# Segment sums of a graph network: two groups in TensorE's column halves, a staging bank, and placing in batches

## The reference

```python
agg_edge = jax.ops.segment_sum(edge_attr, dst, num_segments=12500)     # 12500 x 48
h0 = relu(layernorm(x))
collected = concatenate([h0, agg_edge], axis=1)                         # 12500 x 176
h = silu(collected @ W1 + b1)                                           # 256 wide
h = silu(h @ W2 + b2)
out = x + h0 + (h @ W3 + b3)                                            # 128 wide
```

## Time and profile before

| | |
|---|---|
| median of 3 runs | 367.58 us |
| lowest and highest run | 367.41 and 370.16 us |
| the profiled execution, its own time | 369.57 us |
| its span, first to last instruction | 367.8 us |
| TensorE busy (matmul, load) | 347.2 and 327.8 us |
| VectorE, ScalarE, GpSimd busy | 260.8, 203.1 and 32.6 us |
| moved by DMA | 52.96 MB |

### The profile page before, as it was taken

How to read it: one execution, slowest core, us unless ns; L and a number is a source line. 1 busy time by engine, 2 the same in 40 slices (tenths; PEclk the granted TensorE clock), 3 DMA queues, 4 the chain that set the end, 5 groups by cost and what they waited for, 6 DMA issues and landing times.

```text
span 367.8 us, 11752 instructions
## 1 busy us (share of the span) xinstructions
PE 347.2 (94%) x4336; PEld 327.8 (89%) x4337; DVE 260.8 (71%) x630; ACT 203.1 (55%) x377; POOL 32.6 (9%) x44
## 2 busy tenths in 40 slices
PE   1488999999999999999999999999999999999995
PEld 1387999999999999999999999999999999999994
DVE  6864866976687667866796669766876688666652
ACT  7543466555655566456645565556555654566471
POOL 4011101110111001110111011101110011101100
PEclk9996999999999999999999999999999999999999
DMA  4953756454555455455635554545554555551111
GB/s 136 295 158 83 219 152 177 131 167 134 175 134 165 127 173 168 131 138 172 182 115 152 165 174 123 169 133 175 137 163 127 172 153 149 138 170 28 27 27 47
DMA packets 78757, 52.96 MB, mean 144 GB/s; under 512 B 2482, under 2 KB 78348, under 8 KB 78738
## 3 DMA queue, kind: packets, MB, share of 16 engines
q1 hardware_dynamic: 78738, 52.70, 50.3%
HBM read 46.29 MB, written 6.40 MB: 143 GB/s over the span
## 4 chain that ended last, share of the span: by engine, by line
PE 93%; DVE 4%; issue 2%; POOL 1%; ACTq 0%; DVEq 0%; POOLq 0%; ACT 0%
PE agg_ps L836 41%; PE z L899 14%; PE z L880 7%; PE z L888 6%; PE z L882 6%; PE z L869 3%; PE z L864 3%; PE z L870 3%; PE z L865 3%; PE z L866 3%; PE tp L849 3%; DVE farthest L522 1%; PE z L774 1%; DVE window L505 0%; DVE rel_rows L518 0%
## 5 line engine op out<-in xcount | busy, mean ns | idle before, releaser
L836 PEld LDWEIGHTS agg_ps<-onehot,raw 128*48 128x48 f32 x3128 | 147.8, 128 | 7.3 <-issue 3.6
L836 PE MATMUL agg_ps<-onehot,raw 128*48 128x42 f32 x3128 | 151.1, 217 | 3.3 <-issue 3.3
L714 DVE TENSOR_TENSOR out_t<-z,resid 112x512 f32<-112x512 f32 (+1 forms) x28 | 19.4, 692 | 84.6 <-PE z L899 84.6
L558 DVE TENSOR_TENSOR onehot<-window,rel 128x1176 f32<-128x1176 f32 (+1 forms) x56 | 76.9, 1375 | 0.7
L425 ACT ACTIVATE xn<-x_t,nmr,rstd 112x128 f32<-112x128 f32 (+1 forms) x112 | 46.2, 483 | 36.6 <-DVE nmr L550 29.8
L899 PEld LDWEIGHTS z<-w,h 128*112 128x112 f32 (+1 forms) x448 | 51.7, 176 | 5.3 <-issue 4.5
L377 POOL TENSOR_TENSOR rstd<-vareps,minus_half 112x4 f32<-112x4 f32 (+1 forms) x28 | 28.2, 1008 | 312.0 <-DVE vareps L542 312.0
L899 PE MATMUL z<-w,h 128*112 128x128 f32 (+1 forms) x448 | 54.4, 274 | 0.9 <-ACT h L446 0.9
L446 ACT ACTIVATE h<-z,b2c 128x448 f32<-128x448 f32 (+1 forms) x56 | 32.4, 631 | 26.5 <-PE z L888 26.5
L880 PE MATMUL z<-h_hi,w_hi 128*128 128x448 f32 (+1 forms) x112 | 43.5, 389 | 0.0
L385 ACT ACTIVATE agg_ps<-zeros 48x512 f32<-48x512 f32 x28 | 16.5, 592 | 45.4 <-DVE agg_carry L668 45.4
(11 more groups left out here) (89 smaller groups left out, 341.4 us busy)
## 6 DMA issues: line engine op xcount, KB each, us to landing
raw<-in_edge_attr_dram SPq DMA_DIRECT2D x55, 672.0 KB, 4.6
x_t<-in_x_dram SPq DMA_DIRECT2D x27, 224.0 KB, 2.9
out_dram<-out_t SPq DMA_DIRECT2D x27, 224.0 KB, 2.5
dst_rows<-in_dst_dram SPq DMA_DIRECT2D x1, 768.0 KB
raw<-in_edge_attr_dram SPq DMA_DIRECT2D x1, 480.0 KB, 4.0
out_t<-in_L_gnn_W_dram SPq DMA_DIRECT2D x1, 256.0 KB, 7.0
x_t<-in_x_dram SPq DMA_DIRECT2D x1, 192.0 KB
out_dram<-out_t SPq DMA_DIRECT2D x1, 192.0 KB
```

Source lines behind the costliest of these rows:

```text
L558: return dve.tensor_tensor(onehot[:, slot, 0:n * PER, :], window[:, :].unsqueeze(1).broadcast_to([P, n * PER, WINDOW]), cols.unsqueeze(2). ...
L836: mm = pe.matmul(banks[0:ED, bass.ds(offsets[k], WINDOW)], raw[0:rows, slot, k, j, :], onehot[0:rows, slot, k * PER + j, :], start=False, ...
```

## The change

**Sums.** The matmuls of two neighbouring groups alternate, one writing partitions 0 to 47 and the other partitions 64 to 111 of a new PSUM bank `stage` (`tile_position` (0, 0) and (0, 64)). The 7 pairs of a tile lie side by side in it (7 x 42 columns). Their output addresses are fixed.

**Copy and placing.** ScalarE copies the bank to SBUF (`stage_sums`). TensorE then places each window: one fp32 matmul whose stationary operand is a 112 x 48 slice of the identity and whose moving operand is the staged pair, with the group's offset as output address (`place_batch`). A batch holds the last 3 groups of tile b-1 and the first 11 of tile b, so one wait for a cleared bank serves a batch.

**Order.** TensorE's step becomes: layer 1 of i-1, offsets and sums of i+1, layer 3 of i-2, transposes of i, placing of i+1, layer 2 of i-1. One pair of banks `z` serves layers 1 and 2, so layer 1 waits for the SiLU of the preceding layer 2, and layer 2's loops are turned (output half outside). ScalarE: relu, split_agg, clear_bank, activate2, activate1, normalize, stage_sums. VectorE's step is reordered, and its one-hots run two tiles ahead. SP loads edges three tiles ahead.

**Prologue.** The first destination of every group is loaded by itself, and row set 0 (the first 128 groups) goes through validity, offset, transposes, one-hots and the sums of tile 0 before row sets 1 to 3 are looked at. The formula of the offsets is shorter. TensorE runs 10 and 6 matmuls of the identity whose results nobody reads (`WARM0`, `WARM1`). Tiles 0 and 1 are summed and placed ahead of the loop, which now starts at step 1 and ends in a loop over 4 to 22.

The diff, cut to its core:

```diff
+    PAIRS = GPT // 2
+    STAGED = PAIRS * WINDOW
-    LOOP_FIRST, LOOP_END = 4, 24
+    LOOP_FIRST, LOOP_END = 4, 22
+    WARM0, WARM1 = 10, 6
...
+        staged = sb("staged", [ROW2 + ED, 2, PAIRS, WINDOW])
...
-        z1 = ps("z1", [P, M, BANK])
-        z2 = ps("z2", [P, M, BANK])
+        stage = ps("stage", [P, BANK])
+        z = ps("z", [P, M, BANK])
...
             def step(i, parity):
-                if has(i, -2, NT):
-                    load_edges(i + 2, parity, 0)
+                if has(i, -3, NT):
+                    load_edges(i + 3, 1 - parity, 0)
...
+            def stage_sums(t, parity):
+                act.wait_ge(s_summed, 2 * t + 2)
+                if not isinstance(t, int) or t > 1:
+                    act.wait_ge(s_placed, t)
+                act.activation(staged[:, parity].rearrange("d k w -> d (k w)"), stage[0:ROW2 + ED, 0:STAGED],
+                               ACT.Copy).then_inc(s_staged, 1)
...
             def step(i, parity):
                 if has(i, 1, NT):
                     relu(i - 1)
+                if has(i, 1, NT):
+                    split_agg(i - 1)
                 if has(i, 1, NT - 2):
                     act.wait_ge(s_carried, i)
                     clear_bank(1 - parity)
-                if has(i, 1, NT):
-                    split_agg(i - 1)
-                if has(i, 0, NT):
-                    normalize(i, parity)
                 if has(i, 2, NT):
                     activate2(i - 2)
                 if has(i, 1, NT):
                     activate1(i - 1)
+                if has(i, 0, NT):
+                    normalize(i, parity)
+                if has(i, -1, NT):
+                    stage_sums(i + 1, 1 - parity)
...
-                    for j in range(PER):
-                        mm = pe.matmul(banks[0:ED, bass.ds(offsets[k], WINDOW)],
-                                       raw[0:rows, slot, k, j, :], onehot[0:rows, slot, k * PER + j, :],
-                                       start=False, stop=True, skip_group_check=True)
+                    for j in range(PER):
+                        for side in range(2):
+                            half, k = divmod(2 * pair + side, HALF)
+                            if 2 * pair + side < total:
+                                rows = P if k < counts[half][1] else TAIL_P
+                                at = ROW2 * side
+                                mm = pe.matmul(stage[at:at + ED, pair * WINDOW:(pair + 1) * WINDOW],
+                                               raw[0:rows, 2 * parity + half, k, j, :],
+                                               onehot[0:rows, 2 * parity + half, k * PER + j, :],
+                                               start=(pair == 0 and j == 0), stop=True, skip_group_check=True,
+                                               tile_position=(0, at))
...
+            def place_batch(b, parity, offsets):
+                first, last = batch_of(b)
+                pe.wait_ge(s_staged, b + 1)
+                wait(pe, s_clear, b + 1)
+                for offset, k in zip(offsets, range(first, last)):
+                    group = k % GPT
+                    at = ROW2 * (group % 2)
+                    mm = pe.matmul(banks[0:ED, bass.ds(offset, WINDOW)], ident[0:ROW2 + ED, at:at + ED],
+                                   staged[:, parity if k >= 0 else 1 - parity, group // 2, :],
+                                   start=False, stop=True, skip_group_check=True)
+                    if k == EARLY - 1 and has(b, 1, NT):
+                        mm.then_inc(s_closed, 1)
+                mm.then_inc(s_placed, 1)
...
                 for m in range(M):
                     cols = slice(m * P, (m + 1) * P)
-                    pe.matmul(z1[:, m, 0:n], w1x_hi[:, cols], hT_hi[:, 0:n], start=True, stop=False)
+                    wait(pe, s_h2, M * (t - 1) + m + 1)
+                    pe.matmul(z[:, m, 0:n], w1x_hi[:, cols], hT_hi[:, 0:n], start=True, stop=False)
...
                 if has(i, -1, NT):
                     offsets = offsets_of(i + 1)
+                    sum_tile(i + 1, 1 - parity)
                 if has(i, 2, NT):
                     layer3(i - 2)
                 if has(i, 0, NT):
                     transposes(i, parity)
                 if has(i, -1, NT):
-                    sum_tile(i + 1, 1 - parity, offsets)
+                    place_batch(i + 1, 1 - parity, offsets)
                 if has(i, 1, NT):
                     layer2(i - 1)
```

## The result

| | before | after |
|---|---|---|
| median | 368.34 us (4 runs, those shown ahead among them) | 419.95 us (4 runs, 418.25 to 424.14) |
| span of the profiled execution | 367.8 us | 416.5 us |
| one step, mean of 25 | 12.02 us | 13.77 us |

The ratio is 1.141, with a 95% interval of 1.131 to 1.152: the changed kernel is 14% slower, where 352 us had been forecast, outside the range's upper end of 391.

What follows compares the result with a forecast made beforehand. TensorE's instructions were taken to bound the step: -0.42 us x 26 = -10.9, with -5.0 in the prologue, gave 353.7; the runs' median lying 2.0 lower made it 352 us, range 336 to 391.

Steps and rivals of the forecast that it cites:

- The sums: TensorE's 112 group-sum passes in overlapping column halves: 26 ns each instead of 45.2, saving 2.15 us a step.
- Rival A: At the sums, loads don't overlap between column halves: a pass stays 45.2 ns, kernel 407.6 us; chance 0.17.
- Rival B: At the sums, loads overlap but streams don't: a pass 36 to 42 ns, taken as 39, kernel 389.6 us; chance 0.09.
- Placing and the narrow form: On TensorE, 28 placing passes cost 1.27 us a step; entering and leaving the narrow form a second time adds 0.33.
- One pair of z banks: Layer 1 waits for the preceding layer 2's SiLU on the shared bank: 0.13 us a step, bounds 0 and 0.3.
- The offsets: A load of 1.3 to 3.4 us ahead of the sums, covered by layer 1's ten long queued passes as before.
- sum of a step: TensorE's step changes by -2.15 + 1.27 + 0.33 + 0.13 = -0.42 us, x 26 = -10.9 us.
- Rival C: Overlap holds but the step is stopped elsewhere, 0.4 us more a step; kernel 362.6 us; chance 0.11.
- The copy, ScalarE, VectorE, SP: ScalarE's stage copy takes 0.5 us, covered by layer 3 and the transposes; VectorE's one-hots and SP's loads are in time.
- Prologue: First sums near 11.3 us, layer 1 of tile 0 at 31 to 33; gain 5 us, bounds 1 and 9.
- two offset loads and the flag: In the prologue, between the transposes at 25.5 us and the placing: done at 27.
- the tail: From the last sums to the end: same layers, left at its length.

Runs made afterwards that it cites:

- e1: Changed kernel with every offset load begun 1 or 3 words earlier, at a multiple of 4 words: 363.43 us, ratio 0.988 to the kernel before.
- e5: Kernel before, with odd tiles' offsets loaded from two words earlier so every load starts at a multiple of four words: 362.81 us against 367.55, ratio 0.987.
- e12: Kernel before with only one wait added, layer 1's second half waiting for the SiLU of the preceding layer 2's first half: 406.62 us, ratio 1.107.
- e11: e7 with the offsets of tiles 0 and 1 loaded at the earliest prologue place and `clear_carry(1)` behind ScalarE's copies: 344.60 us, ratio 0.938.
- e3: Changed kernel with constant offsets for tiles 2 to 27, so no per-step loads or register work: 355.01 us, ratio 0.965 to the kernel before.
- e7: Changed kernel with offset loads aligned and ahead of layer 1, x issued first, and VectorE's nmr behind the first low part: 348.34 us, ratio 0.947.
- e2: Changed kernel with the unchanged offset loads placed ahead of layer 1 in TensorE's program: 392.49 us, ratio 1.066 to the kernel before.
- e9: e1 with VectorE making `nmr` ahead of the one-hots: 364.59 us, ratio 0.990 to the kernel before.

## Why the prediction was wrong

**The sums.** Right in mechanism and nearly in size. A pass in column halves costs 22.6 ns, exactly half of the 45.2 of the earlier trace rows, where I took 26; the block takes 2.65 us instead of 5.17, -2.52 against the -2.15 forecast. The floor of 25 ns that I took from the one-column loads is no floor for these. Rivals A and B, which held 26% between them, are both refuted. By the Trainium skill (TensorEngine Tiling (Array Packing), Key Properties) different tiles load and multiply at once, and the runs agree: 22.6 ns in two halves, 45.3 in one. The Trainium skill's page TensorE: Matmul & The Clock Gate, The mechanism, lets a load overlap running matmuls only when its row group differs. Here both groups use all rows and a pass still costs half, so the measurement decides against it for column halves. (Rival B's upper value was misreckoned: by its own slope 42 columns take 44.5 ns and not 42. It changes nothing here.)

**Placing and the narrow form.** 28 passes in 1.38 us, forecast 1.27. Both entries together cost 0.21 us a step more than before, forecast 0.33. Right.

**One pair of z banks.** Layer 1 follows layer 2 without a gap (109.12), the forecast was 0.13 us. As a delay of layer 1 the wait costs nothing. But it is the wait that did the damage elsewhere.

**The offsets.** This is the step that failed: the load "stands in front of the sums instead of layer 3; layer 1's ten long passes in the queue cover it as before". Each half of it was wrong.
- I had read 1332/2329/3370 as a spread. It is two values, by the place of the first word, and the new batches' start (14b - 3) leaves only the long one. e1 and e5 show it: 57 us (some 4.5 of them the slow steps) and 5 us. The median of 2329, between two clusters with nothing near it, was the sign.
- The cover is not "as before". A load covers itself only as far as the sequencer runs ahead, and the new `s_h2` wait at layer 1's second half stops it there: five passes (1.0 us) in front instead of seventeen (3.4). e12 shows it with that wait alone.

Together: 3.34 + 0.3 of register work behind it, less 1.0 of cover, is the 2.6 us of the timeline. With the short load 1.5 + 0.3 - 1.0 = 0.8 (e1: 0.7). My sum of a step had this term at nothing. The wait with short loads (e1) still leaves the kernel 1.2% faster than before. Long loads without the wait were not tried in the changed kernel: with one pair of banks it can't be left out. The odd tiles of the kernel before are such a case: a long load cost 0.19 us there (12.13 against 11.94, gone in e5). So either of the two alone costs little (0.19 us the long load, 0.5 to 0.7 us the wait in e1); the 2.6 us take both. Of the new wait I had asked only how long its own matmul stands, not which instruction behind it used to run early. Rival C did name "the sequencer held", though at the wait for the staged sums, and priced it at up to 0.4 us a step, by the tightness of my count and not by the longest thing behind the wait, 3.4 us in the earlier trace rows.

**The copy, ScalarE, VectorE, SP.** `staged` takes 0.416 us (forecast 0.5) and nobody waits for it. x lands later and `rstd` takes 2.06 us instead of 1.01; both were unforeseen and both are hidden.

**Prologue.** The first sums begin at 11.3, as counted (rows of their line, first and last start):

```profile
L919 PE MATMUL stage<-onehot,raw x3128: 208/213/306, 11.3 to 388.9; 128*48 128x42 f32 x195, 80*48 80x42 f32 x1
```

Then the chain of the changed kernel in order of time goes another way:

```profile
21.56 3.60 PE stage L919 x112
...
25.62 1.65 ACT xn L470 x4
...
27.32 1.01 PE tp L949 x4
28.33 5.06 issue
33.40 2.96 PE agg_ps L936 x34
```

The 5.06 us of "issue" are mostly two loads (1.52 and 3.34) that start only at 27.3, when the wait of the transposes for `xn` is met: the same hold again. I had given "two offset loads and the flag" 1.5 us. Layer 1 of tile 0 begins at 37.46, not at 31 to 33, and the gain of 5 us is not there. e11 loads before that wait: placing at 27.76 and layer 1 at 32.73, within the forecast, though at the low clock (0.50 from 28.6 to 35.3 us, 1.2 GHz). Its timeline:

```profile
27.76 4.22 PE L939 MATMUL agg_ps<-staged,ident 112*48 112x42 f32 x50 [0.49 <-issue]
32.73 0.71 PE L968 MATMUL z<-hT_hi,w1x_hi 128*128 128x448 f32 x1 [0.75 <-issue]
...
36.74 3.15 PE L922 MATMUL stage<-onehot,raw 128*48 128x42 f32 x112
```

**The total.** Rival A's time, 407.6, lay near the measured one, but its reason isn't there. With the stall taken out the kernel takes 355.0 us (e3) or 348.3 (e7), close to my 352, but part of that is luck. A step of e7 takes 11.04 us on the mean of 25, where I had 11.60, 14 us less in all; against it the sums of tile 2 begin at 40.1 where I had 35.3, and the tail, which I had left at its length, is 3.0 us longer.

## What to carry to other kernels

When a wait is added to a queued instruction, look at what the sequencer of that engine would have done early behind it (register loads above all), and price the wait by the longest of these less the work still queued ahead. When the minimum and the maximum of a line are far apart and the median is near neither, list the instructions one by one before taking a value: two values have a cause, and the change may move every instruction to the worse one. Time marked "issue", or a releaser that was done long before, is a reason to look at the sequencer's own rows.

## What the hardware showed beside this

- Loading 14 to 17 words into TensorE's registers took 1.1 to 1.6 us when the first word lay at a multiple of 4 words and 3.34 to 3.80 us when it didn't; beside layer 2 it took 2.0 to 2.4 us (e7) and 3.8 to 4.3 (e2).
- A stall of about 2 us of TensorE was followed by the low clock in some cases and not in others: 6 of 13 in e12, the one of the prologue before; mostly not in the changed kernel (clock 1.00 from 100 to 150 us, with a stall of 2.6 in every step; lower in the steps of tiles 3, 4 and 20). What tells them apart no run settles.
- GpSimd's power took 2.01 to 2.24 us where one of VectorE's one-hots (1.38 us) began with it or up to 0.25 us ahead, and 1.007 alone (e9). It ended 0.86 to 0.88 us after that one-hot in all 26 cases of the changed kernel, as if it had stood still until the one-hot was through. The Trainium skill (SBUF — State Buffer, Who interferes with whom) says that a VectorE instruction with two operands in SBUF, as the one-hot is, contends with a GpSimd one that reads SBUF. The trace agrees.
- Passes in two column halves overlap even in blocks of eight: 27.7 ns against 22.6 in turn and 45.3 in one half.
